# Issuing a shared expert's first weight chunks one at a time in a folded attention loop

## The chip, the cores and the metric

The kernel runs on one core of a Trainium2 chip. The metric is the device time of one execution in microseconds (us), compared as the median over several runs. Times of single instructions come from one profiled execution.

## What is computed

The program is two transformer-like layers on x, 4 batches of 512 tokens by 512 channels, all float32. Each step adds to x: a channel attention, a mixture of experts with a shared expert, a grouped cross attention on a context, and a gated FFN with Hadamard transforms. The change lies in the first of them:

```
query = einsum('bnc,dc->bnd', ctx, Wq) + bq          # ctx: 4 x 512 x 256
key   = einsum('bnc,dc->bnd', ctx, Wk) + bk
attention = softmax(einsum('bnd,bmd->bnm', query, key))
x = x + einsum('bln,bmn->blm', layernorm(x), attention)
```

and at its border to the second, whose shared expert computes for every token

```
shared = silu(xf @ shared_fc1.T) * (xf @ shared_fc2.T) @ shared_proj.T
y = y + sigmoid(xf @ shared_gate_w.T) * shared
```

with 1408 hidden features.

## The kernel before

**Number format.** Every float32 product is three passes on TensorE: each operand is split into a high part (a rounded copy, made by ScalarE) and a low part (the difference, made by VectorE or GpSimd), and `product` at lines 84 to 86 issues high by high, low by high and high by low.

**The attention loop.** `channel_attention` handles 16 tiles of 128 rows (NT = 16, TT = 4 tiles to a batch). Each engine has its own loop over slices i. In slice i TensorE turns the probabilities of tile i (line 745) and the normalised rows of x (line 172), computes the scores of tile i + 2, does the Hadamard product for one block of another matrix, and then the weighted sum of tile i - 4: twelve matmuls of 128x512 at lines 84 to 86 into `ca_ps_x` or `ca_ps_a`. ScalarE makes the exponentials (line 547) and the high parts (lines 555 and 182), VectorE the low parts (lines 640 and 161), maxima and sums (line 650 adds the result to x).

**Work folded into it.** The final FFN's down matrix, 16 blocks of 128x512 (NF = 16), is transformed beside the attention, one block in each slice. For block m: SP loads it into `ca_wd` (line 445 for the first two, line 459 after that); GpSimd multiplies it by a scale in slice m (`scale_wd`, line 487); ScalarE makes its high part in slice m + 1 (`wd_high`, line 561); GpSimd makes the low part in slice m + 1 (`wd_low`, line 493); TensorE does two matmuls in slice m + 2 (lines 753 and 754); ScalarE copies them out (line 567); SP stores the result (line 463). The block has two buffers. On ScalarE, `wd_high` stands in program order ahead of that slice's `attn_high` (line 555), so that a block that is late holds the attention's own work back. GpSimd also does the statistics of the next layer norm once, in slice 14 (`ROOT_STEP`, lines 120 to 126). The keys of the late cross attention are computed in this loop too and are stored by `store_key` (line 450).

**The order on SP.** SP is the queue that issues these transfers. After the inputs, it runs a loop over n from 0 to 15:

```python
for n in range(NF):
    if n + 2 < NF:
        sp.wait_ge(M.wd_ready, n + 1)
        sp.dma_start(wds[n % 2][:], io["wdT"][n + 2])...
    for u in KEYS_AFTER_SCORES.get(n + 1, ()) + KEYS_AT_END.get(n + 1, ()):
        store_key(u)
    sp.wait_ge(M.wd_out, n + 1)
    sp.dma_start(G.had_dram[n], wdz[n % 2][:])...
    if n == SHARED_STEP: ...
```

So step n loads block n + 2, stores the keys that are due, and stores the result of block n.

**The chunks.** The shared expert's weights come in chunks of 128 x 1536 float32 (768 KB). `load_shared` (line 266) loads one of them. The first three go to the three slices `first_slice(G.weights, j)` of one large buffer, which the attention uses as well: its first 2048 columns hold the context (raw), the next 2048 the four stages of the keys. So chunk 0 needs the context's last low part (`M.ctx_ready` at B = 4, made by GpSimd in slice 3), and chunks 1 and 2 also the keys' stores (the last key is stored at step 7). ScalarE splits chunk 0 in slice 16 and chunk 1 in slice 17 (line 279), GpSimd makes their low parts (line 287), and chunk 2 is split in the next stage, `shared_expert`. That stage starts behind the barrier at the end of this block, with the load of chunk 3.

Of the kernel before, what the change touches and what calls it, by code (L numbers as in the profile page):

```python
# [25 lines left out]
B, S, C = 4, 512, 512  # L26
CV = 256
TOK = B * S
NT = TOK // P
# [9 lines left out]
NF = INTER // P  # L39
# [11 lines left out]
GROUP = 4  # L51
# [135 lines left out]
def program(nc, io):  # L187
# [8 lines left out]
    with ExitStack() as top:  # L196
# [8 lines left out]
        with ExitStack() as moe:  # L205
# [20 lines left out]
            with ExitStack() as early:  # L226
                shared_buffers(nc, early, G)
                channel_attention(nc, io, G)
                shared_expert(nc, io, G)
# [35 lines left out]
def load_shared(sp, io, G, j, raw, chunk):  # L265
    sp.dma_start(raw, io["shared_w"][chunk]).then_inc(G.raw_loaded[j], 16)


def store_xn(sp, G, t):
    sp.wait_ge(G.moe_ln.xn_ready, t + 1)  # L270
    xn = G.moe_ln.xn
    sp.dma_start(G.xn_dram[t * P:(t + 1) * P, :], xn[t % len(xn)][:]).then_inc(G.xn_stored[t % len(xn)], 16)
# [17 lines left out]
def first_slice(w, j):  # L290
    return w[:, j * WSLICE:(j + 1) * WSLICE]
# [11 lines left out]
def channel_attention(nc, io, G):  # L303
# [8 lines left out]
    STAGES, PER = 4, EARLY_KEYS  # L312
    KEYS_AFTER_SCORES = {-1: (0,), 0: (1,), 1: (2,), 2: (4,), 3: (7,), 4: (10,), 6: (11,), 7: (13,), 8: (15,)}
    KEYS_AT_END = {1: (3,), 2: (5, 6), 3: (8, 9), 6: (12,), 7: (14,)}
    KEYS = B * PER
    CTX_STEPS = (1, 3)
    KEYS_BEFORE_QK = {1: 1, 2: 11, 3: 16}
    KEYS_IN_X = 8
    SHARED_STEP, STATS_STEP, ROOT_STEP = NF - 6, NT - 7, NT - 2
    with ExitStack() as ctx:  # L320
        sb, ps, sem = scope(nc, ctx, "ca")
        first_sem = sem("first")
# [42 lines left out]
        key_stored = [sem(f"key_stored{i}") for i in range(STAGES)]  # L365
        M = Bag()
# [53 lines left out]
        with nc.Block() as block:  # L420

            @block.sync
            def _(sp):
                def load_ctx(b):
                    if b >= 2:
                        sp.wait_ge(M.ctx_ready, b - 1)
                    sp.dma_start(ctxr[b % 2][:], io["ctxT"][b]).then_inc(ctx_loaded[b % 2], 16)

                sp.dma_start(wr[:], io["ca_w"]).then_inc(M.small_loaded, 16)
                sp.dma_start(bias[:], io["ca_b"]).then_inc(M.small_loaded, 16)  # L430
                load_ctx(0)
                sp.dma_start(G.ident_t[:], io["ident"]).then_inc(M.ident_loaded, 16)
                for b in range(B):
                    sp.dma_start(x[:, TT * b:TT * b + TT, :],
                                 io["x"][b].rearrange("(t p) c -> p t c", p=P)).then_inc(x_loaded[b], 16)
                    if b == 0:
                        at = KC * HPG * D
                        for k in range(KV):
                            sp.dma_start(wkr[:, k, :].rearrange("p (g d) -> p g d", g=PER),
                                         io["xa_w"][0:PER, :, at + k * D:at + (k + 1) * D].rearrange("g p d -> p g d")  # L440
                                         ).then_inc(M.wk_loaded, 16)
                        sp.dma_start(had[:], io["h128"]).then_inc(M.const_loaded, 16)
                        sp.dma_start(wdp[:], io["wscale_dp"].partition_broadcast(P)).then_inc(M.const_loaded, 16)
                        for n in range(2):
                            sp.dma_start(wds[n][:], io["wdT"][n]).then_inc(wd_loaded[n], 16)
                        load_ctx(1)
                def store_key(u):
                    b, g = divmod(u, PER)
                    sp.wait_ge(M.key_out, u + 1)
                    sp.dma_start(G.k_dram[g * B + b], stages[:, u % STAGES, :]).then_inc(key_stored[u % STAGES], 16)  # L450

                for b in range(2, B):
                    load_ctx(b)
                for u in KEYS_AFTER_SCORES[-1] + KEYS_AFTER_SCORES[0]:
                    store_key(u)
                for n in range(NF):
                    if n + 2 < NF:
                        sp.wait_ge(M.wd_ready, n + 1)
                        sp.dma_start(wds[n % 2][:], io["wdT"][n + 2]).then_inc(wd_loaded[n % 2], 16)
                    for u in KEYS_AFTER_SCORES.get(n + 1, ()) + KEYS_AT_END.get(n + 1, ()):  # L460
                        store_key(u)
                    sp.wait_ge(M.wd_out, n + 1)
                    sp.dma_start(G.had_dram[n], wdz[n % 2][:]).then_inc(wd_stored[n % 2], 16)
                    if n == SHARED_STEP:
                        sp.wait_ge(M.ctx_ready, B)
                        for i in range(STAGES):
                            sp.wait_ge(key_stored[i], 16 * (KEYS // STAGES))
                        for j in range(GROUP - 1):
                            load_shared(sp, io, G, j, first_slice(G.weights, j), j)
                for t in range(TT):  # L470
                    store_xn(sp, G, t)
                for i in range(2):
                    sp.wait_ge(wd_stored[i], 16 * (NF // 2))
# [2488 lines left out]
```

## Time and profile before

| | us |
|---|---|
| median of 3 runs | 2298.24 |
| the 3 runs | 2297.0, 2298.24, 2301.62 |
| the profiled execution, its own time | 2297.43 |
| its span | 2295.6 |
| outside the span | 1.8 |
| TensorE busy | 2229.4 (97%) |
| VectorE busy | 1429.4 (62%) |
| ScalarE busy | 1050.1 (46%) |
| GpSimd busy | 470.3 (20%) |

The mean granted TensorE clock of that execution was 0.994 of full speed. In the profile PE is TensorE, PEld its weight load, DVE VectorE, ACT ScalarE, POOL GpSimd, SPq the sequencer that issues the DMAs of SP. A line number is that of the instruction, which for helpers is the helper's line. In a timeline row the figures are start and duration in us, and the square brackets hold the idle time ahead of the instruction with what ended it.

### The profile page before, as it was taken

The numbers are of one execution on the slowest core, as the hardware profiler recorded it, in microseconds if no ns is written. First come the engines' busy times: TensorE is split into PE (matmuls) and PEld (weight loads), VectorE is DVE, ScalarE is ACT, GpSimd is POOL, SyncE is SP. The second block draws the span as 40 slices with busy tenths as digits, with TensorE's granted clock in tenths as the row PEclk, the third lists the DMA queues.
The fourth block names the chain that finished last, engine by engine and source line by source line (L and its number), as shares of the span: only waits on it lengthen the run. The fifth ranks groups of instructions, "written<-read, shape, count | busy, mean of one in ns | idle before, by whom it ended". The sixth has DMA issues, their size and how long they took to land. (4 is left out here: it accounts for less than half of the span.)

```text
span 2295.6 us, 32145 instructions
## 1 busy us (share of the span) xinstructions
PE 2229.4 (97%) x11073; PEld 1851.7 (81%) x11073; DVE 1429.4 (62%) x2979; ACT 1050.1 (46%) x1872; POOL 470.3 (20%) x448
## 2 busy tenths in 40 slices
PE   7989999998999989999999999999998999999999
PEld 5767878887999977888888888888877888888887
DVE  6854365545777775777777767767676555565544
ACT  5432120103565556666666666666664332323321
POOL 4333545401111162100010000100031302121000
PEclk9999999999999999999999999999999999999999
DMA  6321321114877875201001000001001233232331
GB/s 222 130 94 51 106 60 33 33 58 158 286 280 265 274 263 194 63 19 37 25 30 46 27 27 27 27 27 37 28 10 70 83 110 102 92 124 78 110 115 51
DMA packets 92539, 222.33 MB, mean 97 GB/s; under 512 B 9616, under 2 KB 30608, under 8 KB 89360
## 3 DMA queue, kind: packets, MB, share of 16 engines
q1 hardware_dynamic: 84112, 193.65, 24.7%
q0 software_dynamic: 8320, 27.27, 4.7%
q8 instruction: 65, 1.06, 0.2%
q14 instruction: 42, 0.34, 0.0%
HBM read 176.85 MB, written 44.04 MB: 96 GB/s over the span
## 5 line engine op out<-in xcount | busy, mean ns | idle before, releaser
L2054 ACT ACTIVATE route_weights<-route_weights,xa_minus_max 128x512 f32<-128x512 f32 x256 | 184.9, 722 | 193.5 <-DVE xa_minus_max L2202 193.4
L2218 DVE TENSOR_TENSOR xa_late_hi<-xa_ps_t,route_wv_hi 128x512 fp32r<-128x512 f32 x256 | 174.8, 683 | 128.6 <-ACT route_wv_hi L2063 128.5
L1989 POOL TENSOR_TENSOR route_kv_lo<-route_rows,route_kv_hi 128x1024 fp32r<-128x1024 f32 x32 | 76.8, 2400 | 717.4 <-ACT route_kv_hi L2028 717.3
L2063 ACT ACTIVATE route_wv_hi<-xa_ps_t 128x512 fp32r<-128x512 f32 x256 | 151.1, 591 | 105.6 <-PE xa_ps_t L2397 71.1
L2202 DVE CUSTOM_DVE_ANT_0 route_weights<-xa_ps_s,route_mask_bias 128x512 f32<-128x512 f32 x256 | 175.5, 686 | 1.1 <-issue 0.4
L2397 PEld LDWEIGHTS xa_ps_t<-ident,route_weights 128*128 128x128 f32 x1024 | 126.2, 140 | 44.0 <-issue 9.1
L2397 PE MATMUL xa_ps_t<-ident,route_weights 128*128 128x128 f32 x1024 | 153.8, 273 | 5.4 <-DVE xa_late_hi L2218 4.7
L2764 ACT ACTIVATE ffn_silu<-ffn_ps_gate,late_scales 128x512 f32<-128x512 f32 x64 | 44.0, 688 | 248.9 <-PE ffn_ps_gate L86 248.9
L84 PE MATMUL xa_ps_p<-route_wv_hi,route_kv_hi 128*128 128x512 f32 x284 | 119.3, 420 | 4.5 <-DVE xa_late_lo L2240 2.9
L2580 DVE TENSOR_TENSOR route_kv_lo<-route_weights,route_kv_hi 128x1024 fp32r<-128x1024 f32 x42 | 53.7, 1279 | 101.8 <-ACT route_kv_hi L2575 101.6
L1043 ACT ACTIVATE moe_silu<-moe_ps_gate 128x512 f32<-128x512 f32 x44 | 26.2, 596 | 196.8 <-PE moe_ps_gate L86 196.8
L84 PE MATMUL ex_ps_h<-ex_xT_hi,ex_w_hi 128*128 128x256 f32 (+1 forms) x384 | 109.4, 285 | 5.6 <-DVE ex_xT_lo L1625 5.6
L84 PE MATMUL xa_ps_p<-late_xT_hi,late_wq_hi 128*128 128x512 f32 x256 | 111.7, 436 | 2.8 <-DVE late_wq_lo L2187 2.8
L86 PE MATMUL xa_ps_p<-route_wv_hi,route_kv_lo 128*128 128x512 f32 x284 | 112.4, 396 | 0.0
L85 PE MATMUL ex_ps_h<-ex_xT_lo,ex_w_hi 128*128 128x256 f32 (+1 forms) x384 | 108.9, 284 | 0.0
L86 PE MATMUL ex_ps_h<-ex_xT_hi,ex_w_lo 128*128 128x256 f32 (+1 forms) x384 | 108.4, 282 | 0.0
L84 PE MATMUL xa_ps_s<-route_kv_hi,xa_q_hi 128*128 128x512 f32 x256 | 104.6, 409 | 2.9 <-DVE xa_minus_max L2202 2.1
L84 PE MATMUL xa_ps_o<-xa_late_lo 128*128 128x512 f32 x256 | 103.4, 404 | 3.8 <-DVE late_xT_lo L2630 2.4
L2224 DVE TENSOR_TENSOR x<-xa_ps_o,x 128x512 f32<-128x512 f32 x128 | 87.4, 683 | 28.4 <-PE xa_ps_o L86 28.4
L1427 POOL DMA_INDIRECT route_rows<-moe_xn,route_slot_token x40 | 45.5, 1136 | 280.2 <-PE ex_ps_t L1678 232.8
L85 PE MATMUL xa_ps_p<-xa_late_hi,route_kv_hi 128*128 128x512 f32 x256 | 101.8, 398 | 0.0
L86 PE MATMUL xa_ps_s<-route_kv_hi,xa_q_lo 128*128 128x512 f32 x256 | 101.4, 396 | 0.0
(507 smaller groups left out, 6638.1 us busy)
## 6 DMA issues: line engine op xcount, KB each, us to landing
route_weights<-in_ffn_w SPq DMA_DIRECT2D x64, 512.0 KB, 3.7
route_weights<-in_expert_w SPq DMA_DIRECT2D x12, 1408.0 KB, 6.4
ex_w_raw<-in_expert_w SPq DMA_DIRECT2D x12, 1408.0 KB, 6.2
route_weights<-wd_folded SPq DMA_DIRECT2D x64, 256.0 KB, 2.6
moe_y<-ex_y SPq DMA_DIRECT2D x40, 256.0 KB, 3.5
route_weights<-in_expert_w SPq DMA_DIRECT2D x12, 768.0 KB, 8.7
ex_w_raw<-in_expert_w SPq DMA_DIRECT2D x12, 768.0 KB, 8.0
route_weights<-in_xa_w SPq DMA_DIRECT2D x18, 512.0 KB, 3.6
```

The source lines that it names most:

```text
L84: pe.matmul(out, lh, rh, start=start, stop=False)
L85: pe.matmul(out, lh, rl, start=False, stop=False)
L86: return pe.matmul(out, ll, rh, start=False, stop=stop)
L1427: pool.indirect_dma_start(out=G.rows[:, at:at + C], out_offset=None, in_=G.xn_dram, in_offset=bass.IndirectOffsetOnAxis(ap=G.slot_token[:, ...
L1989: pool.tensor_tensor(kvl[b % 2][:], rawkv[b % 2], f32(kvh[b % 2][:]), ALU.subtract).then_inc(M.kv_ready, 1)
L2054: act.activation(prob[slot][:], prob[slot][:], ACT.Exp, bias=nmx[:, slot:slot + 1], scale=-1.0, accum_out=tot[:, slot:slot + 1]).then_inc( ...
L2063: act.activation(PTh[:, :, tt * P:(tt + 1) * P], psT[tt % 2][:].rearrange("p (k n) -> p k n", k=TT), ACT.Copy).then_inc(M.pt_hi, 1)
L2202: dve.tensor_tensor_reduce(out=prob[slot][:], in0=psS[slot % 2][:], in1=maskb[:, b * S:(b + 1) * S], scale=-SCALE, scalar=3.4e38, op0=ALU. ...
L2218: dve.tensor_tensor(PTl[:, :, tt * P:(tt + 1) * P], psT[tt % 2][:].rearrange("p (k n) -> p k n", k=TT), f32(PTh[:, :, tt * P:(tt + 1) * P] ...
L2224: dve.tensor_tensor(x[:, t, :], psO[tt % 2][:], x[:, t, :], ALU.add).then_inc(M.x_added, 1)
L2397: last = pe.transpose(psT[tt % 2][:, k * P:(k + 1) * P], prob[tt][:, k * P:(k + 1) * P], ident)
L2580: dve.tensor_tensor(L.gu_lo[s % 3][:], final_raw(G, s)[0], f32(L.gu_hi[s % 3][:]), ALU.subtract).then_inc(L.gu_ready, 1)
```

## The change

The three loads of chunks 0, 1 and 2 are no longer issued together at the end of step 10, but one at each of the steps 5, 9 and 12, and within the step not at its end but behind the load of block n + 2 and ahead of the key stores and of the store of block n's result. The waits move with them: the one on the context to each of the three steps, the ones on the keys' stores to steps 9 and 12. Nothing is computed otherwise, and the number and sizes of the transfers stay.

```diff
-    SHARED_STEP, STATS_STEP, ROOT_STEP = NF - 6, NT - 7, NT - 2
+    SHARED_STEPS, STATS_STEP, ROOT_STEP = (5, 9, 12), NT - 7, NT - 2
...
                     if n + 2 < NF:
                         sp.wait_ge(M.wd_ready, n + 1)
                         sp.dma_start(wds[n % 2][:], io["wdT"][n + 2]).then_inc(wd_loaded[n % 2], 16)
+                    if n in SHARED_STEPS:
+                        sp.wait_ge(M.ctx_ready, B)
+                        if n != SHARED_STEPS[0]:
+                            for i in range(STAGES):
+                                sp.wait_ge(key_stored[i], 16 * (KEYS // STAGES))
+                        j = SHARED_STEPS.index(n)
+                        load_shared(sp, io, G, j, first_slice(G.weights, j), j)
                     for u in KEYS_AFTER_SCORES.get(n + 1, ()) + KEYS_AT_END.get(n + 1, ()):
                         store_key(u)
                     sp.wait_ge(M.wd_out, n + 1)
                     sp.dma_start(G.had_dram[n], wdz[n % 2][:]).then_inc(wd_stored[n % 2], 16)
-                    if n == SHARED_STEP:
-                        sp.wait_ge(M.ctx_ready, B)
-                        for i in range(STAGES):
-                            sp.wait_ge(key_stored[i], 16 * (KEYS // STAGES))
-                        for j in range(GROUP - 1):
-                            load_shared(sp, io, G, j, first_slice(G.weights, j), j)
```

## Rows read from the trace of the kernel before

**Rows 1.** The page, section 1: busy time, share of the span and instructions.

```profile
PE 2229.4 (97%) x11073; PEld 1851.7 (81%) x11073; DVE 1429.4 (62%) x2979; ACT 1050.1 (46%) x1872; POOL 470.3 (20%) x448
```

**Rows 2.** Busy time by stretch: length, engines' busy us, granted clock, DMA share, GB/s.

```profile
100.00:105.00 5.00, 4.88 (x25) 3.57 (x24) 4.90 (x10) 2.76 (x6) 2.13 (x3) 1.00 0.33 105
110.00:115.00 5.00, 4.16 (x21) 3.04 (x20) 2.72 (x7) 1.26 (x3) 0.00 (x0) 1.00 1.00 368
...
120.00:125.00 5.00, 4.14 (x14) 3.68 (x15) 3.17 (x5) 3.14 (x6) 4.83 (x7) 0.50 0.30 107
```

**Rows 3.** Timeline of TensorE around the gap: start, duration, work, idle ahead.

```profile
112.49 0.47 PE L753 MATMUL ca_ps_wd<-ca_wd_hi,ca_h_r 128*128 128x512 f32 x1 [0.71 <-ACT ca_wd_out L567]
...
115.97 0.39 PE L86 MATMUL ca_ps_x<-ca_attnT_hi,ca_xT_lo 128*128 128x512 f32 x1
120.86 1.09 PE L745 MATMUL ca_ps_a<-ident,route_rows 128*128 128x128 f32 x4 [4.50 <-DVE ca_attnT_lo L640]
...
125.16 0.44 PE L85 MATMUL ca_ps_x<-ca_attnT_lo,ca_xT_hi 128*128 128x512 f32 x1
```

**Rows 4.** Timeline of VectorE: the instruction behind its idle time.

```profile
120.03 0.69 DVE L640 TENSOR_TENSOR ca_attnT_lo<-ca_ps_a,ca_attnT_hi 128x512 fp32r<-128x512 f32 x1 [6.40 <-ACT ca_attnT_hi L555]
```

**Rows 5.** Timeline of ScalarE in slices 13 and 14.

```profile
111.76 0.59 ACT L567 ACTIVATE ca_wd_out<-ca_ps_wd 128x512 f32<-128x512 f32 x1
118.88 0.63 ACT L561 ACTIVATE ca_wd_hi<-ca_wd 128x512 fp32r<-128x512 f32 x1 [6.54 <-POOL ca_wd L487]
119.42 0.58 ACT L555 ACTIVATE ca_attnT_hi<-ca_ps_a 128x512 fp32r<-128x512 f32 x1
```

**Rows 6.** Timeline of GpSimd: blocks 12 and 13 and the next norm's statistics.

```profile
104.60 1.28 POOL L487 TENSOR_TENSOR ca_wd<-ca_wd,ca_wscale_dp 128x512 f32<-128x512 f32 x1 [1.27 <-DMA ca_wd<-in_wdT]
107.49 1.29 POOL L493 TENSOR_TENSOR ca_wd_lo<-ca_wd,ca_wd_hi 128x512 fp32r<-128x512 f32 x1 [1.61 <-ACT ca_wd_hi L561]
117.59 1.26 POOL L487 TENSOR_TENSOR ca_wd<-ca_wd,ca_wscale_dp 128x512 f32<-128x512 f32 x1 [8.81 <-DMA ca_wd<-in_wdT]
...
122.53 1.04 POOL L126 TENSOR_TENSOR moe_ln_rstd<-moe_ln_var_eps,moe_ln_minus_half 128x4 f32<-128x4 f32 x1
```

**Rows 7.** Timeline of SP: the issues of steps 5, 6 and 9 to 12.

```profile
68.16 0.43 SPq L459 DMA_DIRECT2D ca_wd<-in_wdT  x1
68.63 0.93 SPq L450 DMA_DIRECT2D xa_k<-route_weights  x2
...
73.53 0.43 SPq L459 DMA_DIRECT2D ca_wd<-in_wdT  x1
...
96.39 0.43 SPq L459 DMA_DIRECT2D ca_wd<-in_wdT  x1
...
101.83 0.43 SPq L459 DMA_DIRECT2D ca_wd<-in_wdT  x1
106.92 0.32 SPq L463 DMA_DIRECT2D wd_h<-ca_wd_out  x1
107.42 1.31 SPq L266 DMA_DIRECT2D route_weights<-in_shared_w  x3
108.78 0.64 SPq L459 DMA_DIRECT2D ca_wd<-in_wdT  x1
...
112.74 0.43 SPq L459 DMA_DIRECT2D ca_wd<-in_wdT  x1
```

**Rows 8.** Line 266, window 107:109 (the three chunks): issue to landing, us.

```profile
DMA to landing us min/median/max: 4.8/6.9/8.6
```

**Rows 9.** Line 266, window 144:145 (one chunk alone): issue to landing, us.

```profile
DMA to landing us min/median/max: 4.7/4.7/4.7
```

**Rows 10.** Line 459, window 96:102.5 (blocks 11 and 12): issue to landing, us.

```profile
DMA to landing us min/median/max: 2.7/2.7/2.7
```

**Rows 11.** Line 459, window 46:47 (block 4, three key stores behind): issue to landing.

```profile
DMA to landing us min/median/max: 3.7/3.7/3.7
```

**Rows 12.** Line 459, window 108:109.6 (block 13, behind the chunks): issue to landing.

```profile
DMA to landing us min/median/max: 8.7/8.7/8.7
```

## The prediction, made before the changed kernel was run

> **What bounds the kernel now.** I read the page first. TensorE is busy for 97% of the span and no other engine for more than 62% [rows 1], so only time in which TensorE stands still, or runs at a lower clock, can be won. Then the busy time by stretch, around the place of the edit. In an undisturbed stretch of the attention TensorE is busy 4.88 of 5 us at a clock of 1.00; from 120 to 125 us it is busy 4.14 and the granted clock is 0.50 [rows 2], the 1.2 GHz level. Between 110 and 115 the DMA engines are full, at 368 GB/s [rows 2].
>
> The timelines then tell the chain, read backwards. TensorE sits idle for 4.50 us until 120.86, for VectorE's low part at line 640 [rows 3]. VectorE had waited 6.40 us for ScalarE's line 555 [rows 4]. ScalarE does line 555 behind line 561 in its program, and line 561 waited 6.54 us for GpSimd's scaling of block 13 [rows 5]. GpSimd had waited 8.81 us for that block's DMA [rows 6]. SP issued this 256 KB load at 108.78, behind the three chunks of 107.42 [rows 7]; it landed 8.7 us later [rows 12], where blocks 11 and 12 took 2.7 [rows 10]. The chunks themselves landed after 4.8, 6.9 and 8.6 us [rows 8]. The queue works in the order of issue, and block 13 stands at its end. The first chunk is not needed before ScalarE's slice 16, so nothing asks for the three this early.
>
> **What the change takes away.** With nothing in front of it, block 13 is issued as the others are, 0.4 to 0.5 us after the store of 106.92 (block 12: 2.77 us ahead of its scaling, 101.83 to 104.60 [rows 6, 7]). Issued at 107.3, it is there at 110.1, and GpSimd, free since 108.8, scales it until 111.4 [rows 6]. Is anything else late then? ScalarE is at line 567 from 111.76, and takes line 561 about 0.5 us after its start, at 112.2, and line 555 at 112.8 [rows 5]. VectorE is busy until 113.6 (its 6.40 us of idle time end at 120.03 [rows 4]), so the low part ends at 113.6 + 0.7 = 114.3. TensorE is at its weighted sum until the last matmul of 115.97 [rows 3]. So it goes straight on: the whole 4.50 us are won, and between block 13's old and new landing (117.5 and 110.1, a difference of 7.4) and the 4.5 lies a slack of 2.9 us. A block's load in this part of the loop may be 2.9 us late at no cost; I need that figure below.
>
> The second term is the clock. From 120.86 to 125.16, 4.30 us [rows 3], TensorE's work ran at a granted clock of 0.50 [rows 2], behind the gap. At 2.4 GHz the same work takes half: 2.15 us won. The short wait of 0.71 us at 112.49 for line 567 [rows 3] stays: that instruction stands behind an exponential, not behind a DMA. Sum: 4.50 + 2.15 = 6.65 us.
>
> On this second term the Trainium skill (TensorE: Matmul & The Clock Gate, "What's actually happening") says that idleness throttles the array and sustained work releases it, and that where in the program the release falls changes from run to run. The profile has one run, in which the loss was 2.15; by that rule other runs of before may lose less or more, and the gain could differ by a part of it.
>
> **What the change adds.** No instruction is added but a few waits on SP that are met long before. What must be costed are the three new places, each by what it is put ahead of.
>
> Step 5: chunk 0 is issued at 68.6, behind block 7's load of 68.16 and ahead of two key stores [rows 7]. Alone a chunk lands in 4.7 us [rows 9], so at 73.3; the two stores of 256 KB follow it. Of three in a row the first landed at 107.42 + 4.8 = 112.2 and the last at about 108.3 + 8.6 = 116.9 [rows 7, 8], so each further chunk costs 2.35, and each further 256 KB a third of it, 0.8 (block 13 came 0.6 behind the last chunk, at 117.5). Block 8 is issued at 73.53 [rows 7], by when the queue is all but empty. The stages of those two keys are written again slices later. Cost nothing; bound 0 to 1 us.
>
> Step 9: chunk 1 is issued at 96.8, behind block 11 [rows 7], and lands at about 101.8, when block 12 is issued at 101.83. Cost nothing.
>
> Step 12: this is the tight one. Block 14 is issued at 112.74 as before, chunk 2 at 113.2, landing at about 117.9 [rows 7, 9]. SP then reaches the store of block 12 at about 114.4 (TensorE's line 753 of 112.49 [rows 3], plus its pair and the copy) and block 15's load at 114.8, once GpSimd has made block 13's low part. Both queue behind chunk 2: block 15 lands at 117.9 + 2 x 0.7 = 119.3. When does GpSimd want it? Block 14 at 115.5, scaled until 116.8, statistics until 118.3 (1.04 for the longest of its instructions [rows 6]; I allow 1.5), low part of block 14 until 119.6. So block 15 is in time by 0.3 us, and TensorE wants it only in slice 17, three us later. Cost nothing; bound 0 to 1.5 us.
>
> Can a big transfer just behind a small one delay the small one? Beside three key stores block 4 took 3.7 us instead of 2.7 [rows 10, 11], and the first chunk, with two behind it, 4.8 against 4.7 alone [rows 8, 9]. So 0.1 to 1.0 us on blocks 7, 11 and 14, each within the 2.9 us of slack: nothing.
>
> A rule of the Trainium skill speaks against this placement: access to HBM takes 0.2 us on average and 2 us at high load, and this makes up most of a transfer's fixed cost (DMA: Bandwidth & Descriptors, "Latency and other measured facts"). By it each of the three blocks, now read beside a chunk, would land 1.8 us later, and block 14 would use up its slack on GpSimd; the sum would be some 1 us smaller.
>
> What follows the barrier at the end of the attention is triggered by it, not by a clock time, and TensorE bounds most of it [rows 1], so the gain should last to the end. The profiled execution took 2297.43, and would take 2290.8. The median of the runs is 0.8 above it, 2298.24: I forecast 2298.24 - 6.65 = 2291.6 us.
>
> **The rivals.**
> First, only part of the gain is kept: the wait moves. Block 15 behind chunk 2 is the candidate, with block 14's low part next to it; or the other runs lose less by the clock than the profiled one. For it: 0.3 us of slack on GpSimd is thin. Against: TensorE wants the block three us later. Price: the clock's 2.15 falls out, or 1.5 to 3 us of new wait: the gain is 3.5 to 5, the time 2293.2 to 2294.7. Chance 0.17.
>
> Second, the gap does not go, because something else that I took as early is late at 113 to 116 us, or the gain is lost in a later stage (the next stages begin with waits and with low clock of their own). Against: all the releasers of the gap are one chain that ends at one DMA [rows 3 to 7]. Time 2296.5 to 2299. Chance 0.08.
>
> Third, slower. The mechanism: transfers in flight share the engines instead of following one another, so a block's load that is issued 0.4 us ahead of a chunk lands with it. There are now three such places, blocks 7, 11 and 14, where before there was none. The point from which it decides is the slack of 2.9 us: a landing above 5.6 us. Lower price: landing at 4.7 + 0.4 = 5.1 costs nothing. Upper price: all three land like block 13 now, at 8.7 [rows 12], and each costs 6.65: +19.95 - 6.65, or 2311.5. Against: the first of three chunks landed at 4.8 and not with the last at 8.6 [rows 8]. Chance 0.03.
>
> That the change doesn't do what it says is no rival of weight: the context's low parts are done in slice 3 and the last key is stored at step 7, so the waits at 5, 9 and 12 can't hold SP.
>
> **How the numbers follow.** The forecast has 0.72, the rivals 0.17, 0.08 and 0.03. A measurement of this kernel can tell about 0.2%, 4.6 us, from no change. The forecast's own range is 2289.5 to 2293.5: bounds of 0 and 1.5 us for what is added, and about 1.5 for the medians (the three runs shown spread over 4.6 us). The first rival's range is taken in, so the range is 2289.0 to 2295.5. The gain of 6.65 is 2 us above the bound of 4.6; noise can carry some of the first case below it, and the first rival lies on both sides of it. Faster: 0.68 of the first case and 0.06 of the first rival, 0.74. Slower: 0.03. Same: the rest, 0.23.
>
> **What would show it right or wrong.** In the profile after, SP issues three chunks at about 68.6, 96.8 and 113.2, and block 13 at 107.3 with a landing of 2.7 to 3. GpSimd's wait for it shrinks from 8.81 to about 1.3 us; TensorE has no gap above 1 us between 111 and 125 and a granted clock of 1.00 there; the work from the chunk's split on stands 6 to 7 us earlier. It is wrong if a wait of GpSimd for block 14 or 15 of over 2 us appears, if TensorE waits at line 753 or 745 in slices 15 to 17, or if the attention ends 6 us earlier and the span does not.

## The result, and the profile after

The changed kernel takes 2292.77 us (median of 11 runs, 2289.78 to 2296.33), the kernel before 2298.24 (11 runs, 2296.28 to 2301.62). The ratio is 0.9973, with a 95% interval of 0.9966 to 0.9981. That is 5.5 us less in the medians, and between 4.4 and 7.8 us less by the interval. (The quotient of the two medians is 0.9976; ratio and interval here are those on record for the two sets of runs.) The forecast was 2291.6, the range 2289.0 to 2295.5. The gain is past the 4.6 us that the prediction called the least that can be told from no change, but the interval begins just below it. Two further comparisons of the same pair gave 0.9977 (0.9968 to 0.9986) and 0.9976 (0.9967 to 0.9984). In the experiments four single executions took 3079 to 7918 us, of the kernel before as of others; the ratios leave them out, the medians do not.

The head of the page of the changed kernel, for [rows 1]:

```profile
span 2291.0 us, 32147 instructions
...
PE 2227.5 (97%) x11073; PEld 1851.7 (81%) x11073; DVE 1430.7 (62%) x2979; ACT 1050.4 (46%) x1872; POOL 471.5 (21%) x448
```

Busy time by stretch in the changed kernel, columns as in [rows 2]: length, busy time of PE, PEld, DVE, ACT and POOL, granted clock, DMA share, GB/s.

```profile
110.00:115.00 5.00, 4.17 (x22) 3.11 (x21) 3.94 (x7) 3.25 (x7) 2.17 (x3) 1.00 0.55 160
115.00:120.00 5.00, 5.00 (x27) 3.87 (x25) 2.32 (x4) 2.09 (x4) 4.14 (x6) 1.00 0.71 263
120.00:125.00 5.00, 4.59 (x25) 3.76 (x25) 2.37 (x5) 3.67 (x8) 4.11 (x4) 1.00 0.14 52
```

The DMA engines are no longer full in the first row, TensorE is busy throughout the second, and the clock is 1.00 in all three. SP's timeline in the changed kernel answers to [rows 7]:

```profile
67.41 0.43 SPq L459 DMA_DIRECT2D ca_wd<-in_wdT  x1
67.89 0.47 SPq L266 DMA_DIRECT2D route_weights<-in_shared_w  x1
68.40 0.91 SPq L450 DMA_DIRECT2D xa_k<-route_weights  x2
...
95.49 0.43 SPq L459 DMA_DIRECT2D ca_wd<-in_wdT  x1
96.11 0.33 SPq L266 DMA_DIRECT2D route_weights<-in_shared_w  x1
...
106.40 0.43 SPq L459 DMA_DIRECT2D ca_wd<-in_wdT  x1
...
111.85 0.43 SPq L459 DMA_DIRECT2D ca_wd<-in_wdT  x1
112.45 0.33 SPq L266 DMA_DIRECT2D route_weights<-in_shared_w  x1
...
113.83 0.43 SPq L459 DMA_DIRECT2D ca_wd<-in_wdT  x1
```

This execution ran 0.9 us ahead of the first one long before the place of the edit (slice 14's line 753 at 111.60 against 112.49), so times are compared from there. GpSimd's scaling of blocks 13, 14 and 15, for [rows 6] (the line numbers behind the edit are one higher):

```profile
109.25 1.28 POOL L488 TENSOR_TENSOR ca_wd<-ca_wd,ca_wscale_dp 128x512 f32<-128x512 f32 x1 [1.37 <-DMA ca_wd<-in_wdT]
...
114.65 1.28 POOL L488 TENSOR_TENSOR ca_wd<-ca_wd,ca_wscale_dp 128x512 f32<-128x512 f32 x1 [1.31 <-DMA ca_wd<-in_wdT]
...
119.37 1.28 POOL L488 TENSOR_TENSOR ca_wd<-ca_wd,ca_wscale_dp 128x512 f32<-128x512 f32 x1 [0.69 <-DMA ca_wd<-in_wdT]
```

The wait for block 13 is 1.37 us instead of 8.81. TensorE's timeline in the changed kernel, for [rows 3], with the first matmul of the shared expert:

```profile
111.60 0.47 PE L754 MATMUL ca_ps_wd<-ca_wd_hi,ca_h_r 128*128 128x512 f32 x1 [0.70 <-ACT ca_wd_out L568]
...
115.07 0.39 PE L86 MATMUL ca_ps_x<-ca_attnT_hi,ca_xT_lo 128*128 128x512 f32 x1
115.31 0.60 PE L746 MATMUL ca_ps_a<-ident,route_rows 128*128 128x128 f32 x4
...
135.54 0.47 PE L84 MATMUL moe_ps_gate<-moe_xT_first_hi,moe_w_first_hi 128*128 128x512 f32 x1 [1.35 <-DVEq L1065]
```

and that last instruction in the kernel before:

```profile
143.15 0.47 PE L84 MATMUL moe_ps_gate<-moe_xT_first_hi,moe_w_first_hi 128*128 128x512 f32 x1 [1.35 <-DVEq L1064]
```

From slice 14's line 753 to the first matmul of the shared expert it is 143.15 - 112.49 = 30.66 us before and 135.54 - 111.60 = 23.94 after. This stretch is called the tail below. It became 6.72 us shorter; the forecast sum was 6.65. The wait of 0.7 us for line 568 stayed, as was said. Steps 5 and 9 lie ahead of the tail. There, from 60 to 111 us, the trace lists no wait of TensorE in either kernel.

### The profile page after: what moved, and what is told of

It reads as the page before. It is cut to its first block and busy times, and to the rows that moved or that the text cites. A ratio compares the mean times of both kernels' runs of the same rounds, so it can differ in the third digit from the quotient of the medians.

```text
span 2291.0 us, 32147 instructions
## 1 busy us (share of the span) xinstructions
PE 2227.5 (97%) x11073; PEld 1851.7 (81%) x11073; DVE 1430.7 (62%) x2979; ACT 1050.4 (46%) x1872; POOL 471.5 (21%) x448
## 5 line engine op out<-in xcount | busy, mean ns | idle before, releaser
L2398 PEld LDWEIGHTS xa_ps_t<-ident,route_weights 128*128 128x128 f32 x1024 | 126.2, 140 | 44.1 <-issue 9.1
```

Of the source, the lines that this page charges most:

```text
L2398: last = pe.transpose(psT[tt % 2][:, k * P:(k + 1) * P], prob[tt][:, k * P:(k + 1) * P], ident)
```

## The experiments

Each kernel below was run 7 to 12 times, unless a single execution is said. The theory: transfers of the queue land in the order of issue, block 13 stood behind the chunks, 2.9 us of its lateness are free, the rest stops TensorE, and the low clock behind the stop costs some 2 us more.

**The ceiling: the three loads without their bytes.** At the old place of the kernel before:

```diff
                         for j in range(GROUP - 1):
-                            load_shared(sp, io, G, j, first_slice(G.weights, j), j)
+                            c = slice(2 * C, 3 * C) if j == 2 else slice(0, 16)
+                            sp.dma_start(first_slice(G.weights, j)[:, c],
+                                         io["shared_w"][j][:, c]).then_inc(G.raw_loaded[j], 16)
```

> The kernel before, with the three loads at their old place at the end of step 10, but with almost no bytes: 16 of 1536 columns of chunks 0 and 1 and the last 512 columns of chunk 2, so 256 KB in all instead of 2304 KB. The rest of the three chunks is left out, so the first group of the shared expert works on other data. Theory A: block 13 is late by one 256 KB transfer, 0.6 to 0.8 us, within the slack of 2.9, so no gap and no low clock; 6.65 us below the kernel before, and level with the changed kernel within 1 us, if the three new places cost nothing. Theory B' (the new places cost something): this kernel is 1 to 3 us faster than the changed one.

Measured: ratio 0.9971 (0.9960 to 0.9982), median 2292.89 us, and a tail of 136.26 - 112.32 = 23.94 us, to the hundredth that of the changed kernel. The changed kernel, run beside it:

> The changed kernel once more, as the yardstick of this group. Theory A (the order of issue: block 13 stood behind 2.3 MB, its lateness beyond a slack of 2.9 us stopped TensorE for 4.5 us and brought its clock down for another 2.15): 6.65 us below the kernel before, ratio 0.9971. Theory B (a part of the gain is lost in later stages, as the first profile's difference of only 4.6 us in the span suggests): 4 to 5 us, ratio 0.9980.

It gave 0.9977, median 2293.3, and a tail of 136.75 - 112.83 = 23.92. So it takes the bytes ahead of block 13 to make the gap, and the three new places cost nothing in the attention: theory B' falls by the tails. The two ratios alone would not tell 1 us.

One part of the expectation was wrong. Block 13 was to be 0.6 to 0.8 us late without the bytes. GpSimd waited much longer:

```profile
108.61 1.51 SPq L459 DMA_DIRECT2D ca_wd<-in_wdT  x1
```

```profile
112.58 1.28 POOL L489 TENSOR_TENSOR ca_wd<-ca_wd,ca_wscale_dp 128x512 f32<-128x512 f32 x1 [3.96 <-DMA ca_wd<-in_wdT]
```

A wait of 3.96 us against 1.37 in the changed kernel is 2.6 us of lateness: 1.5 because SP reaches the issue later, behind three others, and 1.1 because the block lands after 3.9 us and not 2.8. Of block 13's lateness before, 7.4 us, the bytes made 4.8. The other 2.6 stay just inside the 2.9 us that are free, so TensorE does not show them.

**How much lateness is free: one, two or three chunks ahead of block 13.** From the changed kernel, one chunk is put back:

```diff
-    SHARED_STEPS, STATS_STEP, ROOT_STEP = (5, 9, 12), NT - 7, NT - 2
+    SHARED_STEPS, STATS_STEP, ROOT_STEP = (5, 9), NT - 7, NT - 2
...
                     sp.dma_start(G.had_dram[n], wdz[n % 2][:]).then_inc(wd_stored[n % 2], 16)
+                    if n == NF - 6:
+                        sp.wait_ge(M.ctx_ready, B)
+                        for i in range(STAGES):
+                            sp.wait_ge(key_stored[i], 16 * (KEYS // STAGES))
+                        for j in (2,):
+                            load_shared(sp, io, G, j, first_slice(G.weights, j), j)
```

> Chunks 0 and 1 at steps 5 and 9 as in the change, chunk 2 back at the end of step 10, ahead of block 13. Theory A (each chunk ahead of it delays block 13 by some 2.35 us plus its issue time, and 2.9 us are free): block 13 lands about 2.8 us late, TensorE waits 0 to 0.3 us, the clock stays: 6.5 us below the kernel before, ratio 0.9972. Theory E (no slack; every delay of the block stops TensorE): a wait of 2.8 us, 3.9 us below the kernel before.

Then two (`(5,)` above, and `for j in (1, 2)`):

> Chunk 0 at step 5, chunks 1 and 2 back at the end of step 10. Theory A: block 13 lands 5.2 us late, less 2.9 of slack: TensorE waits 2.3 us. If its clock stays at 1.00, 4.35 us below the kernel before (ratio 0.9981); if it falls as behind the wait of 4.5 us, 2.2 below (ratio 0.9990). Theory E: a wait of 5.2 us and a time at that of the kernel before or above.

GpSimd's scaling of block 13 and the start of TensorE's slice 15, with one chunk back:

```profile
113.72 1.29 POOL L494 TENSOR_TENSOR ca_wd<-ca_wd,ca_wscale_dp 128x512 f32<-128x512 f32 x1 [4.75 <-DMA ca_wd<-in_wdT]
```

```profile
117.03 0.63 PE L752 MATMUL ca_ps_a<-ident,route_rows 128*128 128x128 f32 x4 [0.48 <-DVE ca_attnT_lo L647]
```

and with two back:

```profile
115.18 1.28 POOL L494 TENSOR_TENSOR ca_wd<-ca_wd,ca_wscale_dp 128x512 f32<-128x512 f32 x1 [6.50 <-DMA ca_wd<-in_wdT]
```

```profile
118.48 0.90 PE L752 MATMUL ca_ps_a<-ident,route_rows 128*128 128x128 f32 x4 [2.23 <-DVE ca_attnT_lo L647]
```

The ratios are 0.9980 (0.9970 to 0.9990) with one back and 0.9989 (0.9979 to 0.9999) with two. Theory E falls; the waits say it most clearly, together with those of the next experiment and of [rows 3, 6]:

| chunks ahead of block 13 | GpSimd's wait | TensorE's wait | difference | tail |
|---|---|---|---|---|
| none (changed kernel) | 1.37 | 0 | | 23.94 |
| three without their bytes | 3.96 | 0 | | 23.94 |
| one | 4.75 | 0.48 | 4.27 | 24.72 |
| three, issued 5 us earlier | 5.42 | 1.16 | 4.26 | 25.39 |
| two | 6.50 | 2.23 | 4.27 | 27.94 |
| three (kernel before) | 8.81 | 4.50 | 4.31 | 30.66 |

TensorE waits for what goes beyond 4.27 us of GpSimd's wait. 1.37 of these are there anyway, so the slack is 4.27 - 1.37 = 2.9 us, as forecast. The tail shows the clock as well. With one chunk back, 0.78 us are lost for a wait of 0.48; with two, 4.00 for 2.23. The rest is 0.30 and 1.77. The 0.30 is lost at a clock of 1.00: a wait costs a little more than its own length, which is called the restart below. The 1.77 is mostly the clock. Busy time by stretch, with two back:

```profile
115.00:120.00 5.00, 2.77 (x15) 2.23 (x13) 1.89 (x3) 2.36 (x5) 3.99 (x5) 0.87 0.19 71
120.00:125.00 5.00, 4.87 (x18) 3.57 (x16) 1.85 (x3) 2.55 (x6) 4.17 (x5) 0.79 0.33 116
```

The mean clocks of 0.87 and 0.79 are 1.3 and 2.1 us at the 1.2 GHz level: 3.4 us behind a wait of 2.2, and half of it, 1.7 us, lost.

**Is it the order or the spreading: all three at step 10, behind block 12.** The block of the change stands as it is, but with

```diff
-                    if n in SHARED_STEPS:
+                    if n == 10:
...
-                        j = SHARED_STEPS.index(n)
-                        load_shared(sp, io, G, j, first_slice(G.weights, j), j)
+                        for j in range(GROUP - 1):
+                            load_shared(sp, io, G, j, first_slice(G.weights, j), j)
```

> All three chunks together at step 10 as before, but behind the load of block 12 instead of behind the store of block 10 (which is 4.6 us earlier). Theory A: the last chunk lands 9.5 us after the first issue, at about 110.9 us, block 13 behind it at 112.3, 3.2 us later than undisturbed; with 2.9 us of slack TensorE waits 0.3 us (bounds 0 to 1) and keeps its clock: 6 us below the kernel before, ratio 0.9974. Theory C (what helps is the spreading over three steps; three chunks in a row always stop the loop): a gap of over 3 us and a time within 2 us of the kernel before.

Measured: ratio 0.9986 (0.9978 to 0.9995). SP issues the chunks at 102.52. TensorE's slice 15:

```profile
117.56 0.63 PE L745 MATMUL ca_ps_a<-ident,route_rows 128*128 128x128 f32 x4 [1.16 <-DVE ca_attnT_lo L640]
```

Its clock is 1.00 from 110 to 125 us. Theory C falls: three chunks in a row, moved by one load and 5 us, lose 1.45 us of tail and not 6.72. But the wait is 1.16 us and not my 0.3: the three cost 0.8 us more in the queue than I had counted. The run times show less of the gain than the tail does: 3.2 us (1.1 to 5.1 by the interval), where the expectation had 6.

**The order inside a step: each chunk ahead of its block.** The changed kernel, with the new lines above the load of block n + 2:

```diff
+                    if n in SHARED_STEPS:
+                        ...
                     if n + 2 < NF:
                         sp.wait_ge(M.wd_ready, n + 1)
                         sp.dma_start(wds[n % 2][:], io["wdT"][n + 2]).then_inc(wd_loaded[n % 2], 16)
-                    if n in SHARED_STEPS:
-                        ...
```

> The changed kernel, but at steps 5, 9 and 12 each chunk stands ahead of that step's own block and not behind it. Theory A (in the order of issue): blocks 7, 11 and 14 land after 5.2 to 5.6 us instead of 2.7 to 3.0. Blocks 7 and 11 stay within the slack; block 14 has only 0.8 us of it, since GpSimd makes the next norm's statistics too: TensorE waits some 2 us at line 753, and the time is 2 us above the changed kernel, ratio 0.9982 to the kernel before. Theory D (chunk and block share the engines whichever is first): blocks land as in the changed kernel, and the time is level with it.

Issue to landing of the load of block 11 in that kernel (window 96:97):

```profile
DMA to landing us min/median/max: 4.8/4.8/4.8
```

and of block 14 (window 113:114):

```profile
DMA to landing us min/median/max: 5.4/5.4/5.4
```

In the changed kernel both take 2.7. TensorE's timeline with the chunks ahead:

```profile
107.38 0.47 PE L754 MATMUL ca_ps_wd<-ca_wd_hi,ca_h_r 128*128 128x512 f32 x1 [0.74 <-ACT ca_wd_out L568]
...
123.14 0.47 PE L754 MATMUL ca_ps_wd<-ca_wd_hi,ca_h_r 128*128 128x512 f32 x1 [2.30 <-POOL ca_wd_lo L494]
```

Ratio 0.9989 (0.9979 to 0.9998), median 2296.51. Theory D falls: what stands first in the queue lands first. The wait at line 754 is the one forecast, 2.3 us; the tail, 138.66 - 112.83 = 25.83, is 1.89 us longer than the changed kernel's. Block 7 landed after 5.8 us (window 68:69) and cost TensorE nothing. One wait was not forecast: 0.74 us a slice after block 11, ahead of the tail, where I had called the block's delay free. The slack of 2.9 us was read for the way to line 745 alone. Behind block 11 ScalarE waits 1.65 us for GpSimd at line 562, VectorE 0.90 us for line 556, and so the slice's exponential comes 0.7 us late, with line 568 behind it (at 105.97, against 104.74 in the changed kernel, which ran 0.5 us ahead). In slice 15, behind block 13, no exponential follows any more (the last starts at 111.08 in the kernel before).

**The far end: all three at step 12, behind block 14** (as the kernel with step 10, with 12):

> All three chunks at step 12 behind block 14. Now block 15 is the one behind them. Theory A: it lands at about 123.3 us in place of 119.4, 3.9 late; GpSimd's low part of it is then ready at 126.6, and TensorE, which gets to it at 123.7, waits 2.9 us: 3.8 us below the kernel before with the clock at 1.00 (ratio 0.9984), 2 us if it falls. If block 15 has more slack than I think: level with the changed kernel.

```profile
128.03 0.47 PE L753 MATMUL ca_ps_wd<-ca_wd_hi,ca_h_r 128*128 128x512 f32 x1 [2.77 <-POOL ca_wd_lo L493]
```

The wait is 2.77 us, at the instruction and of the size expected; the tail, 139.83 - 112.89 = 26.94, is 3.72 us shorter than before, against 3.8. The granted clock stays at 1.00 behind this wait and behind the 2.30 us of the kernel above, although it fell behind the 2.23 us with two chunks back. Yet the ratio is 0.9998 (0.9989 to 1.0008), so at most 2.5 us of the 3.72 reached the end. In the profiled execution a part goes soon behind the tail: TensorE waits 2.18 us in the shared expert, where the kernel before has 1.4 to 1.6, and 3.4 us at the 1.2 GHz level follow.

**The clock term alone: the gap filled.** The kernel before, with

```diff
                     if i < NT:
+                        if i == NT - 1:
+                            pe.wait_ge(M.exp_done, NT - 1)
+                            for r in range(18):
+                                pe.matmul(psS[0][:], hadr[:], wh[:].rearrange("p a b c -> p (a b c)"),
+                                          start=True, stop=True)
                         turn(i)
```

> The kernel before, with its three loads at their old place, and 18 extra matmuls of 128x512 on TensorE ahead of the turn of tile 15, into a bank that nobody reads; they take 18 x 0.235 = 4.2 us, nearly the idle 4.5. Nothing that the output needs is changed. Theory A (the low clock follows from the idle time): the granted clock stays at 1.00 from 112 to 127 us, the wait for block 13 stays, and the time is 2.15 us below the kernel before, ratio 0.9991. Rival: the clock falls for another reason, or the extra work delays what follows; the time is level or above.

TensorE's timeline of that kernel:

```profile
116.28 4.37 PE L785 MATMUL ca_ps_s<-ca_wqk_hi,ca_h_r 128*128 128x512 f32 x18
...
121.06 0.63 PE L745 MATMUL ca_ps_a<-ident,route_rows 128*128 128x128 f32 x4 [0.41 <-DVE ca_attnT_lo L640]
```

and its busy time by stretch:

```profile
115.00:120.00 5.00, 5.00 (x23) 4.02 (x22) 0.00 (x0) 0.93 (x2) 1.51 (x2) 1.00 0.47 177
120.00:125.00 5.00, 4.59 (x24) 3.49 (x23) 3.17 (x5) 3.26 (x7) 4.83 (x6) 1.00 0.31 107
```

GpSimd still waits 8.87 us for block 13. The clock stays at 1.00, and the tail is 141.41 - 112.58 = 28.83, 1.83 us shorter than before. Of the 2.22 us lost beside the wait 0.39 are left, near the 0.30 of the restart; the rest was the clock's, shown in the trace. The ratio, 0.9992 (0.9980 to 1.0004), has the same size (1.8 us) but does not exclude no change.

**Does the kernel before vary, and where is the last microsecond?** The kernel before against itself, and two single executions:

> The kernel before, unchanged, against itself: it shows what a comparison can resolve, and one more profile of the gap. Locally the change gave 6.7 us twice, but the medians differ by 5.5 and 5.0. Theory F (the low clock behind the gap varies from run to run): the gap is again 4.5 us, and the stretch at 0.50 behind it is sometimes 3.4 us long and not 6.8, which gives TensorE 1 to 1.7 us less loss. Theory G (nothing varies there; the missing 1 us is noise of the later stages): gap 4.5, low clock 6.8 us each time. The ratio should be 1.000 within 0.001.

> A second look at the kernel before, for the low clock behind the gap. Theory F: of three looks at least one with a loss by the clock under 1.8 us. Theory G: 2.1 to 2.2 us as in the first profile.

> A third look at the kernel before. Theory F and theory G as for the second: a loss by the clock under 1.8 us in one of the three, or 2.1 to 2.2 us in all.

> The changed kernel a third time, for the size of the gain over more runs. Local gain up to the first matmul of the shared expert 6.7 us by both theories if the kernel before loses 2.2 us by its clock; no gap and a clock of 1.00 in the attention. Ratio 0.9971 if all of it arrives at the end, 0.9977 as in the last comparison if a microsecond does not.

The kernel before against itself gave 0.9998 (0.9989 to 1.0007), so a comparison resolves about 2 us here. Its three new profiles have waits of 4.58, 4.43 and 3.80 us in slice 15 and tails of 143.83 - 112.92 = 30.91, 144.27 - 113.00 = 31.27 and 142.09 - 112.53 = 29.56. Less the wait and the changed kernel's 23.94, the clock and restart cost 2.39, 2.90 and 1.82, where the first profile had 2.22. Theory G (2.1 to 2.2 each time) falls. The mean of the four tails is 30.60, hence a local gain of 6.66. The third new profile, from 120 us:

```profile
120.00:125.00 5.00, 4.80 (x18) 3.91 (x19) 2.54 (x5) 2.40 (x5) 4.83 (x7) 0.66 0.43 150
```

In the stretches of 5 us around it the clock is 1.00, so 3.4 us were at the low level. In the first profile it was 6.8 us, by the stretch from 120 us [rows 2] and the two beside it:

```profile
115.00:120.00 5.00, 1.36 (x6) 0.76 (x4) 0.00 (x0) 1.12 (x3) 1.67 (x2) 0.84 0.46 174
125.00:130.00 5.00, 4.59 (x19) 3.40 (x19) 1.60 (x3) 2.79 (x5) 3.43 (x3) 0.98 0.28 105
```

Stretches of half a microsecond show where the low level begins and ends, and so how much of it falls into work and how much into the wait:

| profile | low level, us | TensorE starts again | works at the low level | half of that | lost beside the wait |
|---|---|---|---|---|---|
| before, first | 118.4 to 125.2 | 120.86 | 4.38 | 2.19 | 2.22 |
| before, second | 119.3 to 126.2 | 121.36 | 4.80 | 2.40 | 2.39 |
| before, third | 120.4 to 127.2 | 121.30 | 5.90 | 2.95 | 2.90 |
| before, fourth | 121.4 to 124.8 | 120.20 | 3.41 | 1.71 | 1.82 |
| two chunks back | 118.7 to 122.1 | 118.48 | 3.41 | 1.71 | 1.77 |

Half the work time at the low level gives each loss to within 0.12 us. Theory F is thus borne out: the loss varies, one profile has 3.4 us at the low level in place of 6.8, and its loss by the clock, 1.7 us, is just under the mark of 1.8. But the variation goes both ways.

The changed kernel's third tail is 136.65 - 112.69 = 23.96. Its ratio, 0.9976, does not tell 6.7 us from 5.5. That execution has a stretch of low clock which the other two of the changed kernel lack:

```profile
150.00:155.00 5.00, 4.92 (x19) 4.34 (x20) 4.12 (x9) 3.24 (x6) 0.00 (x0) 0.67 0.06 22
```

It follows a wait of 2.3 us in the shared expert's second matmul group (line 172, for VectorE, whose chain begins with a small table's DMA); the other two have 1.9 and 1.5 us there, the four profiles of the kernel before 1.4 to 1.6.

## Why the prediction was right, and what of it was not

- **The chain** (chunks, block 13, lines 487, 561, 555, 640, 745) is shown: taking away the bytes alone removes the whole gap, and with one, two and three chunks TensorE's wait is GpSimd's less 4.3 us each time.
- **The first term, 4.50 us**, is confirmed in the trace. The slack of 2.9 us read from block 13's two landings came out at 2.9. It does not hold for every consumer: behind block 11 a delay of some 2.5 us cost 0.74, by way of an exponential.
- **The second term, 2.15 us**, was the right size and rightly computed, but is no constant: 2.22, 2.39, 2.90 and 1.82 in four profiles. It was luck that the first profile lay near their mean of 2.33; one profile gives this term only to within some 0.6 us. The Trainium skill (TensorE: Matmul & The Clock Gate, "What's actually happening") says that where the clock rises changes from run to run. The trace agrees: counted from the end of the wait it rises after 4.4, 4.8, 5.9 and 4.6 us.
- **The three new places** cost nothing: no wait of TensorE behind steps 5 and 9, and nothing in the tail (23.94, 23.92 and 23.96 against 23.94 without the bytes). Step 12 was called tight by 0.3 us on GpSimd; in fact GpSimd waited 0.69 us for block 15, and TensorE did not feel it. In the first profile of the changed kernel the chunks landed after 5.8, 4.5 and 5.6 us, where the sum had 4.7.
- **A small transfer ahead of a big one** is not delayed: blocks 7, 11 and 14 landed after 2.8, 2.7 and 2.7 us, where the prediction had allowed 0.1 to 1.0 us more than 2.7. The Trainium skill's rule of 2 us at high load (DMA: Bandwidth & Descriptors, "Latency and other measured facts") would, by the prediction's estimate of 1.8 us more, have made it 4.5; the trace shows nothing of this.
- **That the gain lasts to the end** is the step that is only half borne out. Three comparisons give 5.3 to 6.2 us (0.9973, 0.9977, 0.9976), each interval holds 6.7, and all lie below it. The profiled executions differ by more: with starts aligned to the first profile of the kernel before, the three changed ones end 3.7, 6.2 and 2.1 us ahead of it, after 6.7 in each tail. So the prediction's own sign of being wrong (the attention ends 6 us earlier and the span does not) half appeared. From the shared expert's first matmul to the end of the span the kernel before takes 2152.2 to 2153.1 us in its four profiles, the changed kernel 2155.5, 2153.0 and 2157.1, and the one without the bytes 2156.1. Paired instruction by instruction, the traces drift apart at a few places only, the stretches at 140 to 160, 400 to 560, 800 to 900 and 1700 to 1760 us; the four profiles of the kernel before drift from each other, by up to 2.4 us, at the last three too. Whether the change makes the losses there likelier stays open; three profiles do not show it.

Of the rivals, the moved wait did not appear, though it can be made: all three chunks at step 12 give 2.77 us of it. The second, a gain lost in a later stage, appeared in part, as said. The slower case needed landings above 5.6 us in three places. With the chunks put ahead they were 5.8, 4.8 and 5.4, and the result was still below the kernel before.

No version tried beats the changed kernel. The one without the bytes is the ceiling for this edit, and the two are level in the tail.

## What to carry to other kernels

A transfer that nobody needs soon is cheap only if no small, urgent one stands behind it in the queue; look for the block whose landing goes from 3 to 9 us and follow it to the bounding engine. Read the slack from a row (lateness of the landing less idle time of the bound engine) for each consumer of the transfer, and keep every batch of bytes below it; moving three loads by one place in the program won 5.3 of the 6.7 us of the tail before any spreading. The issues on the queue count too: three of them, nearly without bytes, made block 13 2.6 us late. Where a change makes TensorE stop or start, price the clock behind the stop separately and take it from several profiles: here the clock stayed up behind waits of 2.3 and 2.8 us, one of 2.2 cost 1.8 us more than itself, and ones of 3.8 to 4.6 cost 1.8 to 2.9 more.

## What the runs showed of the hardware that was not expected

- The length of a wait did not settle what the clock did behind it. It stayed at 1.00 behind waits of 1.16, 2.30 and 2.77 us. One of 2.23 was followed by 3.4 us at the 1.2 GHz level, one of 3.80 by 3.4 too. Behind waits of 4.50, 4.58 and 4.43 us the low level lasted 6.8 us each time, but began 2.4, 2.0 and 0.9 us before the wait's end; with the wait of 3.80 it began 1.2 us after it.
- With the gap filled by 18 matmuls whose result nobody reads the clock stayed up, and the kernel lost 1.8 us less in its tail while doing 4.4 us more work.
- Each chunk of 768 KB ahead of a block added not one fixed sum to GpSimd's wait but 3.4 us (the first, with its issue), 1.75 (the second) and 2.3 (the third): 1.37, 4.75, 6.50 and 8.81.
- SP needed 0.43 us to issue the routing constants' broadcast in ten of the fourteen profiled executions, but 0.83 us in the first of the changed kernel, 0.84 with the chunks ahead, 1.22 with all three at step 12 and 1.33 without the bytes; the table behind it came later by as much. In the changed kernel's third profile the issue took 0.42, but the table itself landed after 4.0 us in place of 2.9 to 3.3. These five are the ones with a long wait in the shared expert (1.9, 1.9, 2.2, 2.5 and 2.3 us, against 1.3 to 1.6), and in all but the first of them 3.4 us at the 1.2 GHz level followed.
